# A graph-attention layer: gathers in waited bursts of two groups in place of spaced and paced gathers

## The chip, the cores and the metric

The kernel runs on one core of one Trainium2 chip. The metric is the device time of one launch in microseconds (us), the median over runs. The engines are TensorE (PE, with its weight loads PEld), VectorE (DVE), ScalarE (ACT), GpSimd (POOL) and SyncE (SP); DMAs are issued from SP, ACT and POOL.

## The reference

One layer of edge attention on a graph of 6250 nodes and 100,000 edges, 8 heads of 12, with a residual and a norm. The edges are sorted by destination, the sources are random.

```python
Q_h = (x @ Wq + bq).reshape(N, H, D)
K_h = (x @ Wk + bk).reshape(N, H, D)
V_h = (x @ Wv + bv).reshape(N, H, D)
E = (edge_attr @ We + be).reshape(-1, H, D)
score = K_h[src] * Q_h[dst] / sqrt(D) * E
score = exp(clip(score.sum(-1, keepdims=True), -5.0, 5.0))
wV = segment_sum(V_h[src] * score, dst)
Z = segment_sum(score, dst)
return layernorm(x + (wV / (Z + 1e-6)).reshape(N, H * D))
```

## The kernel before

**Tables.** TensorE computes keys, values and queries of all nodes in 50 tiles of 128 nodes; ScalarE copies them out of PSUM and SP stores them in two tables in HBM, kv_table (rows of 192 floats, 768 bytes) and q_table. Meanwhile GpSimd gathers the x rows of the sources of the first 8 groups, and TensorE computes their keys and values straight from them, so that these groups need no table.

**Groups.** The edges are taken in 196 groups (`GROUPS`) of 4 tiles (`GROUP_TILES`) of 128 edges; the last group has 2 tiles, 782 tiles in all. For each tile GpSimd issues one indirect DMA (L493, in `gather`) that fetches 128 rows of kv_table by the tile's source numbers into the ring `kv` of 16 groups (`KV_RING`). Each ring slot has its own semaphore, `e_kv[slot]`, which a gather raises by 16 when its rows have landed.

**What each engine does for a group.** TensorE, in this order in one iteration of its loop: `features_and_queries` (L1023 edge features, L1030 queries of the edges by a one-hot product), for the group two before it `turn` (L1041, transposes of their product), and for the group five before it `segment_sums` (L1055). ScalarE makes the one-hot matrix (L588, L591), copies the features (L597) and takes the exponentials (L602, L603). VectorE multiplies queries and features (L751), multiplies that with the gathered keys (L761, `times_keys`; this is the operation that waits for `e_kv`), sums over the heads (L768), clips (L775), weighs the gathered values (L782, `weigh_v`, which raises `e_msg`) and adds the sums of a window of 80 nodes to the accumulator (L797). SP loads edge features, relative rows and query windows, in rings of 8 groups. TensorE raises `e_e` (L1023), `e_q` (L1030), `e_turn` (L1041) and `e_seg` (L1055), once for each group.

**The order on GpSimd.** It has nothing to do but the gathers. After every gather stands a spacer (L500, in `space`): a memset of a tile that no one reads, which also waits for the memset before it. Groups 0 to 7 (`EARLY`) gather x rows; then GpSimd waits until all tables are stored; groups 8 to 15 go out without a wait; groups 16 to 31 wait, once for each group, until the slot's old contents have been used (`e_msg`); from group 32 on (`PACED_FROM`) each of the four gathers of a group waits for a signal of TensorE:

```python
pool.wait_ge(*((e_seg, group - 3), (e_e, ahead + 1),
               (e_q, ahead + 1), (e_turn, group + 1))[t])
```

where `ahead` is `group + 2`. The other engines' rows are ordered by hand; finished nodes are normalised and stored while the groups go on (`steps_at`). Of the three paths (`by_path`) these inputs take the streamed one, `windowed(True)`.

Of the kernel before, what the change touches and what calls it, by code (L numbers as in the profile page):

```python
# [31 lines left out]
F32 = mybir.dt.float32  # L32
# [7 lines left out]
P = 128  # L40
# [6 lines left out]
GROUP_TILES = 4  # L47
GROUP = GROUP_TILES * P
GROUPS = -(-N_EDGES // GROUP)
# [4 lines left out]
QUADS = GROUPS // QUAD  # L54
WINDOW = 80
EARLY = 8
PACED_FROM = 32

NODE_TILES = -(-N_NODES // P)
TABLE_TILES = NODE_TILES + 1  # L60
# [19 lines left out]
KV_RING, EA_RING, REL_RING, QWIN_RING, PICK_RING, MSG_RING = 16, 8, 8, 8, 4, 4  # L80
# [9 lines left out]
TURNED, WEIGHED, SUMMED, ADDED = 2, 3, 5, 5  # L90
# [4 lines left out]
def tiles_of(group):  # L95
    return min(GROUP_TILES, TILES - group * GROUP_TILES)


def edges_in(tile):
    return min(P, N_EDGES - tile * P)  # L100
# [37 lines left out]
def build(nc, xT, x_rows, src_cols, dst_cols, dst_rows, eaT, weights, biases, ones, out):  # L138
# [9 lines left out]
    assert FINISHED_AFTER[STREAMED_STEPS - 2] + LAG_DIVIDE < GROUPS + 1 == FINISHED_AFTER[STREAMED_STEPS - 1] + LAG_DIVIDE  # L148
    assert STREAMED_STEPS == STEPS - 1 and ADDED == 5 and TURNED == 2 and WEIGHED == 3
    assert SUMS * FINAL_TILES + WINDOW <= 512 and LAG_TRANSPOSE == SUMMED + 2  # L150
    assert KV_RING > 2 * SUMMED and PACED_FROM >= KV_RING
    assert EARLY < KV_RING and tiles_of(EARLY) == GROUP_TILES


# [6 lines left out]
    with ExitStack() as ctx:  # L161
        def sb(name, shape, dt):
            return ctx.enter_context(nc.sbuf_tensor(name, shape, dt))
# [4 lines left out]
        def sem(name):  # L168
            return ctx.enter_context(nc.semaphore(name))
# [66 lines left out]
        rows_f = acc_t[0:PAIRS, 0:2 * GROUP].rearrange("p (j e) -> p j e", j=2)  # L236


        spacer = sb("spacer", [P, 128], F32)
        g_src = sb("g_src", [P, GROUP_TILES], U32)  # L240
        g_dst = sb("g_dst", [P, GROUP_TILES], U32)
        g_dst_f = sb("g_dst_f", [P, GROUP_TILES], F32)
# [58 lines left out]
        e_kv = [sem(f"e_kv{i}") for i in range(KV_RING)]  # L301
# [5 lines left out]
        e_e = sem("e_e")  # L307
        e_q = sem("e_q")
# [3 lines left out]
        e_turn = sem("e_turn")  # L312
# [4 lines left out]
        e_msg = sem("e_msg")  # L317
        e_seg = sem("e_seg")
        e_acc = sem("e_acc")
        e_space = sem("e_space")  # L320
        g_free = sem("g_free")
        g_idx = sem("g_idx")
        g_step = sem("g_step")
# [31 lines left out]
        def path_of(eng):  # L355
            eng.wait_ge(r_ready, 1)
            return eng.value_load(path_i[0:1, 0:1], min_val=GENERAL, max_val=STREAMED)
# [6 lines left out]
        def all_tables_stored(eng):  # L364
            for i in range(UNITS_IN_RING):

                eng.wait_ge(d_table[i], 32 * len(range(i, UNITS, UNITS_IN_RING)))

        def by_path(eng, path, windowed, general):

            with eng.If(path == STREAMED):
                windowed(True)
            with eng.Else():
                with eng.If(path == WINDOWED):
                    windowed(False)
                with eng.Else():
                    general()
# [103 lines left out]
        @block.gpsimd  # L481
        def _(pool):
            nc.gpsimd.memset(ident[:], 0.0).then_inc(c_id0, 1)
            pool.wait_ge(c_id0, 1)
            nc.gpsimd.affine_select(out=ident[:], in_=ident[:], compare_op=ALU.not_equal, fill=1.0, base=0,
                                    pattern=[[-1, P]], channel_multiplier=1).then_inc(c_ident, 1)
            nc.gpsimd.iota(iota_i[:], pattern=[[1, SPAN]], base=0, channel_multiplier=0).then_inc(c_iota, 1)
            nc.gpsimd.iota(part_i[:], pattern=[[1, 1]], base=0, channel_multiplier=1).then_inc(c_iota, 1)

            def gather(rows, table, group, t, semaphore):  # L490
                tile = group * GROUP_TILES + t
                n = edges_in(tile)
                pool.indirect_dma_start(rows[0:n, :], None, table,  # L493
                                        bass.IndirectOffsetOnAxis(ap=src_idx[0:n, tile:tile + 1], axis=0)
                                        ).then_inc(semaphore, 16)

            def space(tile):
                if tile:
                    pool.wait_ge(e_space, tile)
                nc.gpsimd.memset(spacer[:], 0.0).then_inc(e_space, 1)  # L500

            pool.wait_ge(l_src_early, 16)
            for group in range(EARLY):
                for t in range(GROUP_TILES):
                    gather(kv[:, group, t, 0:DIM], x_rows, group, t, e_kv[group])
                    space(group * GROUP_TILES + t)
            pool.wait_ge(l_src, 16)
            all_tables_stored(pool)
            path = path_of(pool)

            def windowed(streamed):
                for group in range(EARLY, GROUPS):
                    slot, ahead = group % KV_RING, min(group + 2, GROUPS - 1)
                    if KV_RING <= group < PACED_FROM:
                        pool.wait_ge(e_msg, group - KV_RING + 1)
                    for t in range(tiles_of(group)):
                        if group >= PACED_FROM:
                            pool.wait_ge(*((e_seg, group - 3), (e_e, ahead + 1), (e_q, ahead + 1), (e_turn, group + 1))[t])
                        gather(kv[:, slot, t, :], kv_table, group, t, e_kv[slot])
                        space(group * GROUP_TILES + t)  # L520

            def general():
                pool.wait_ge(l_dst, 16)
                pool.wait_ge(x_kv, 2 * EARLY)
                with pool.Fori(0, GROUPS) as group:
                    pool.wait_ge(g_free, group + 1)
                    cols = bass.ds(group * GROUP_TILES, GROUP_TILES)
                    nc.gpsimd.tensor_copy(g_src[:], src_idx[:, cols]).then_inc(g_idx, 1)
                    nc.gpsimd.tensor_copy(g_dst[:], dst_idx[:, cols]).then_inc(g_idx, 1)
                    pool.wait_ge(g_idx, group * 2 + 2)  # L530
                    pool.sem_inc(g_step, 1)
                    for t in range(GROUP_TILES):
                        pool.indirect_dma_start(
                            kv[:, 0, t, :], None, kv_table,
                            bass.IndirectOffsetOnAxis(ap=g_src[:, t:t + 1], axis=0)).then_inc(g_gather, 16)
                        pool.indirect_dma_start(
                            g_q[:, t, :], None, q_table,
                            bass.IndirectOffsetOnAxis(ap=g_dst[:, t:t + 1], axis=0)).then_inc(g_gather, 16)

            by_path(pool, path, windowed, general)  # L540


# [605 lines left out]
```

## Time and profile before

| | |
|---|---|
| median of 2 runs | 1071.3 us (1071.09 to 1071.5) |
| span of the profiled execution | 1231.7 us |
| time of the profiled execution around its span | not shown by the profile |
| GpSimd busy | 919.8 us (75%) |
| TensorE busy, mean granted clock | 824.3 us (67%), 0.81 |
| VectorE busy | 595.7 us (48%) |
| ScalarE busy | 457.8 us (37%) |
| rows gathered by GpSimd's queue | 75.28 MB, 23.9% of the 16 DMA engines' span |

The profile is of one execution. Its rows give the start and length of each instruction; the length of a gather on GpSimd is the making of its descriptors, and its rows land later. The granted clock is TensorE's, 1.0 for 2.4 GHz and 0.5 for 1.2 GHz. The profiled execution is 160 us longer than the timed ones.

### The profile page before, as it was taken

To read this page: it belongs to the slowest core of one execution; us is meant where nothing else is said; L and a number is where in the kernel's file an instruction comes from. 1 tells how busy PE (TensorE), PEld (TensorE's weight loads), DVE (VectorE), ACT (ScalarE), POOL (GpSimd) and SP (SyncE) were. 2 spreads that over 40 slices of the span, in tenths; PEclk is the share of its full clock that TensorE was granted. 3 is DMA by queue.
4 is the path that set the end of the run, shared out by engine and by line. 5 is a ranking of instruction groups with operands and counts; after the bars stand their busy time and mean duration, and the time that the engine had idled before them with its cause. 6 is when DMAs were issued, how large, how long until landed. Compare 5 with 4: busy or idle time off the path is not lost.

```text
span 1231.7 us, 13818 instructions
## 1 busy us (share of the span) xinstructions
PE 824.3 (67%) x3375; PEld 455.9 (37%) x3375; DVE 595.7 (48%) x1583; ACT 457.8 (37%) x1094; POOL 919.8 (75%) x1572
## 2 busy tenths in 40 slices
PE   6518565986676666667676667666767676776763
PEld 4415232543343333333333334333333333333433
DVE  5104344954444464445444545445554545454645
ACT  3206232743343343333333334333434343433331
POOL 8882777167878778778787787887777877877783
PEclk9757787988877888887888787887878877878885
DMA  9922344454545445445444444444444444444321
GB/s 245 277 77 77 104 126 109 137 145 120 144 116 138 125 112 131 125 111 127 122 121 125 108 135 117 120 132 120 111 130 125 128 127 112 121 130 126 92 77 51
DMA packets 124525, 153.29 MB, mean 124 GB/s; under 512 B 57885, under 2 KB 92191, under 8 KB 124436
## 3 DMA queue, kind: packets, MB, share of 16 engines
q0 software_dynamic: 37008, 75.28, 23.9%
q1 hardware_dynamic: 80608, 73.74, 21.7%
q10 hardware_dynamic: 6822, 3.31, 1.0%
q8 instruction: 31, 0.51, 0.2%
q14 instruction: 56, 0.46, 0.1%
HBM read 142.26 MB, written 9.98 MB: 124 GB/s over the span
## 4 chain that ended last, share of the span: by engine, by line
POOL 37%; PE 22%; issue 16%; another core or an unknown queue 10%; DVE 6%; DMA 6%; ACT 2%; SPq 0%; DVEq 0%; POOLq 0%
POOL kv L493 30%; POOL spacer L500 7%; DMA kv<-kv_table,src_idx 5%; PE ps_eq L1030 4%; PE ps_eq L1023 4%; PE ps_qe_seg L1055 3%; PE ps_last L1055 3%; PE ps_eq_qe L1023 2%; PE ps_qe_seg L1041 2%; PE ps_eq_qe L1030 1%; PE ps_eq_qe L1041 1%; DVE ps_last L768 1%; DVE node_stage L743 1%; DMA w_all<-biases_in 1%
## 5 line engine op out<-in xcount | busy, mean ns | idle before, releaser
L493 POOL DMA_INDIRECT kv<-kv_table,src_idx x750 | 714.2, 952 | 285.5 <-issue 114.7
L602 ACT ACTIVATE ps_last<-clipped 128x32 f32<-128x32 f32 x196 | 39.4, 201 | 542.4 <-issue 397.2
L1030 PE MATMUL ps_eq<-pick_t,q_win 128*96 128x512 f32 (+1 forms) x262 | 169.5, 735 | 78.7 <-ACT e_t L597 58.4
L761 DVE TENSOR_TENSOR kq<-kv,ps_qe_seg 128x384 f32<-128x384 f32 x98 | 53.9, 550 | 260.7 <-DMA kv<-kv_table,src_idx 195.7
L1023 PE MATMUL ps_eq<-ea,w_all 128*96 128x512 f32 (+1 forms) x262 | 172.5, 747 | 8.1 <-issue 7.4
L500 POOL MEMSET spacer<- 128x128 f32 x782 | 172.8, 221 | 2.7 <-remote 2.2
L761 DVE TENSOR_TENSOR kq<-kv,ps_eq_qe 128x384 f32<-128x384 f32 x98 | 54.1, 552 | 238.3 <-DMA kv<-kv_table,src_idx 175.5
L1055 PE MATMUL ps_qe_seg<-node_stage 128*104 128x80 f32 x784 | 116.2, 306 | 54.5 <-issue 28.9
L1055 PE MATMUL ps_last<-node_stage 128*104 128x80 f32 x780 | 108.2, 292 | 49.3 <-issue 24.2
L588 ACT ACTIVATE distance<-rel_bc,neg_part 80x512 bf16<-80x512 bf16 x196 | 138.4, 706 | 1.8 <-issue 0.6
L1055 PEld LDWEIGHTS ps_qe_seg<-node_stage 128*104 128x104 f32 x784 | 105.2, 218 | 64.6 <-issue 49.6
L591 ACT ACTIVATE pick_t<-distance 80x512 f32<-80x512 bf16 x196 | 123.2, 629 | 6.2
L1055 PEld LDWEIGHTS ps_last<-node_stage 128*104 128x104 f32 x780 | 97.7, 205 | 58.0 <-issue 33.5
L1030 PEld LDWEIGHTS ps_eq<-pick_t,q_win 128*96 128x96 f32 x262 | 46.4, 199 | 195.0 <-issue 194.4
L597 ACT COPY e_t<-ps_eq 96x512 f32<-96x512 f32 x131 | 74.3, 567 | 92.6 <-remote 58.2
L768 DVE TENSOR_REDUCE ps_last<-kq 128x32 f32<-128x384 f32 x196 | 107.6, 549 | 0.1
L782 DVE TENSOR_TENSOR node_stage<-kv,ps_last 128x384 f32<-128x384 f32 x196 | 106.3, 542 | 0.0
L1041 PE MATMUL ps_qe_seg<-ident,qe_t 96*128 96x96 f32 x390 | 60.0, 285 | 65.9 <-issue 41.2
L1030 PE MATMUL ps_eq_qe<-pick_t,q_win 128*96 128x512 f32 x130 | 82.6, 722 | 31.7 <-issue 15.8
L1041 PEld LDWEIGHTS ps_qe_seg<-ident,qe_t 96*128 96x128 f32 x390 | 48.3, 164 | 146.1 <-issue 103.4
L751 DVE TENSOR_TENSOR qe_t<-e_t,ps_eq 96x512 f32<-96x512 f32 x131 | 88.3, 674 | 17.5 <-PE ps_eq L1030 8.9
L1041 PEld LDWEIGHTS ps_eq_qe<-ident,qe_t 96*128 96x128 f32 x392 | 48.3, 160 | 125.9 <-issue 92.3
(90 smaller groups left out, 788.2 us busy)
## 6 DMA issues: line engine op xcount, KB each, us to landing
ea<-ea_t_in SPq DMA_DIRECT2D x196, 192.0 KB
rel_bc<-rel_rows_dram SPq DMA_DIRECT2D x196, 80.0 KB
kv<-kv_table,src_idx POOLq DMA_INDIRECT x750
q_win<-q_table SPq DMA_DIRECT2D x196, 30.0 KB
kv_table<-node_stage SPq DMA_DIRECT2D x5, 576.0 KB
x_both<-x_t_in SPq DMA_DIRECT2D x5, 480.0 KB, 8.9
x_both<-x_rows_in ACTq DMA_DIRECT2D x10, 240.0 KB
out<-node_stage SPq DMA_DIRECT2D x11, 192.0 KB
```

Of the source, the lines that this page charges most:

```text
L493: pool.indirect_dma_start(rows[0:n, :], None, table, bass.IndirectOffsetOnAxis(ap=src_idx[0:n, tile:tile + 1], axis=0)).then_inc(semaphore ...
L500: nc.gpsimd.memset(spacer[:], 0.0).then_inc(e_space, 1)
L588: nc.scalar.activation(distance[:, b, 0:n], rel_bc[:, slot, 0:n], ACT.Abs, bias=neg_part[0:WINDOW, :]).then_inc(e_dist, 1)
L591: nc.scalar.activation(pick_t[0:WINDOW, group % 3, 0:n], distance[:, b, 0:n], ACT.Relu, bias=1.0, scale=-1.0).then_inc(e_pt, 1)
L751: nc.vector.tensor_tensor(qe_t[:, group % QE_RING, 0:n], e_t[:, group % 2, 0:n], ps_eq[(2 * group + 1) % 3][0:DIM, 0:n], ALU.mult).then_in ...
L761: nc.vector.tensor_tensor(kq[:, group % 2, 0:n, :], kv[:, slot, 0:n, 0:DIM], ps_qe[group % 2][:, 0:n * DIM].rearrange("p (t d) -> p t d", ...
L768: nc.vector.tensor_reduce(score[:, group % 2, 0:n, :], kq[:, group % 2, 0:n, :].rearrange("p t (h d) -> p t h d", h=HEADS), axis=AX_X, op= ...
L782: nc.vector.tensor_tensor(m[:, :, 0:DIM].rearrange("p t (h d) -> p t h d", h=HEADS), kv[:, group % KV_RING, 0:n, DIM:2 * DIM].rearrange("p ...
L1023: nc.tensor.matmul(ps_eq[2 * group % 3][0:DIM, 0:n], w_e, ea[:, slot, 0:n], start=True, stop=True).then_inc(e_e, 1)
L1030: nc.tensor.matmul(ps_eq[(2 * group + 1) % 3][0:DIM, 0:n], q_win[:, slot, :], pick_t[:, group % 3, 0:n], start=True, stop=True).then_inc(e ...
L1041: last = nc.tensor.transpose(ps_qe[group % 2][:, t * DIM:(t + 1) * DIM], qe_t[:, group % QE_RING, t * P:(t + 1) * P], ident[0:DIM, 0:DIM])
L1055: last = nc.tensor.matmul(ps_seg[group % 2][0:SUMS, 0:WINDOW], msg[:, group % MSG_RING, t, :], pick[:, group % PICK_RING, t, :], start=(t ...
```

## The change

The spacers and the four signals of TensorE go. Gathers go out in bursts of two groups (`BURST`), eight gathers one behind the other, and behind each burst GpSimd waits until both groups have landed (`landed`, on `e_kv` of both slots). The wait for the ring slot (`e_msg`) stands ahead of every group from 16 on. Behind the last burst there is no wait for its landing. The other four engines' programs are unchanged.

```diff
-PACED_FROM = 32
+BURST = 2
...
-        spacer = sb("spacer", [P, 128], F32)
...
-        e_space = sem("e_space")
...
-            def space(tile):
-                if tile:
-                    pool.wait_ge(e_space, tile)
-                nc.gpsimd.memset(spacer[:], 0.0).then_inc(e_space, 1)
+            def landed(group, tiles):
+
+                slot = group % KV_RING
+                before = sum(tiles_of(g) for g in range(slot, group, KV_RING))
+                pool.wait_ge(e_kv[slot], 16 * (before + tiles))
 
             pool.wait_ge(l_src_early, 16)
             for group in range(EARLY):
                 for t in range(GROUP_TILES):
                     gather(kv[:, group, t, 0:DIM], x_rows, group, t, e_kv[group])
-                    space(group * GROUP_TILES + t)
+                if group % BURST == BURST - 1:
+                    for g in range(group - BURST + 1, group + 1):
+                        landed(g, GROUP_TILES)
...
                 for group in range(EARLY, GROUPS):
-                    slot, ahead = group % KV_RING, min(group + 2, GROUPS - 1)
-                    if KV_RING <= group < PACED_FROM:
+                    slot = group % KV_RING
+                    if group >= KV_RING:
                         pool.wait_ge(e_msg, group - KV_RING + 1)
                     for t in range(tiles_of(group)):
-                        if group >= PACED_FROM:
-                            pool.wait_ge(*((e_seg, group - 3), (e_e, ahead + 1), (e_q, ahead + 1), (e_turn, group + 1))[t])
                         gather(kv[:, slot, t, :], kv_table, group, t, e_kv[slot])
-                        space(group * GROUP_TILES + t)
+                    if group % BURST == BURST - 1 and group < GROUPS - 1:
+                        for g in range(group - BURST + 1, group + 1):
+                            landed(g, GROUP_TILES)
```

On GpSimd at the start of the program (the gathers of x rows), the kernel before has a spacer behind each gather:

```order
L493 DMA kv<-x_rows_in,src_idx 128x96 [waits l_src_early]
L500 MEMSET spacer 128x128
L493 DMA kv<-x_rows_in,src_idx 128x96
L500 MEMSET spacer 128x128 [waits e_space]
L493 DMA kv<-x_rows_in,src_idx 128x96
L500 MEMSET spacer 128x128 [waits e_space]
```

The changed kernel has eight gathers in a row, and the first of each next eight waits for the landing of two groups:

```order
L491 DMA kv<-x_rows_in,src_idx 128x96 [waits l_src_early]
L491 DMA kv<-x_rows_in,src_idx 128x96 x7
L491 DMA kv<-x_rows_in,src_idx 128x96 [waits e_kv1,e_kv0]
L491 DMA kv<-x_rows_in,src_idx 128x96 x7
L491 DMA kv<-x_rows_in,src_idx 128x96 [waits e_kv3,e_kv2]
L491 DMA kv<-x_rows_in,src_idx 128x96 x7
```

The spacers are gone, and the waits of the early part moved from the spacer's own semaphore to the landings.

On GpSimd in the steady stage, the kernel before has for one group four gathers that wait for TensorE's signals, with the spacers between them:

```order
L493 DMA kv<-kv_table,src_idx 128x192 [waits e_seg]
L500 MEMSET spacer 128x128 [waits e_space]
L493 DMA kv<-kv_table,src_idx 128x192 [waits e_e]
L500 MEMSET spacer 128x128 [waits e_space]
L493 DMA kv<-kv_table,src_idx 128x192 [waits e_q]
L500 MEMSET spacer 128x128 [waits e_space]
L493 DMA kv<-kv_table,src_idx 128x192 [waits e_turn]
L500 MEMSET spacer 128x128 [waits e_space]
```

The changed kernel has there, for three groups (`e_msg` is the ring slot, `e_kv` with a number the landing of a slot):

```order
L491 DMA kv<-kv_table,src_idx 128x192 [waits e_msg,e_kv3,e_kv2]
L491 DMA kv<-kv_table,src_idx 128x192 x3
L491 DMA kv<-kv_table,src_idx 128x192 [waits e_msg]
L491 DMA kv<-kv_table,src_idx 128x192 x3
L491 DMA kv<-kv_table,src_idx 128x192 [waits e_msg,e_kv5,e_kv4]
L491 DMA kv<-kv_table,src_idx 128x192 x3
```

No wait for TensorE is left there; every second group begins with the wait for the landing of the two before it, and all gathers behind it stand in the same queue.

## Rows read from the trace of the kernel before

**Rows 1.** The page: busy time of each engine, and the chain that ended last
```profile
PE 824.3 (67%) x3375; PEld 455.9 (37%) x3375; DVE 595.7 (48%) x1583; ACT 457.8 (37%) x1094; POOL 919.8 (75%) x1572
...
POOL kv L493 30%; POOL spacer L500 7%; DMA kv<-kv_table,src_idx 5%; PE ps_eq L1030 4%; PE ps_eq L1023 4%; PE ps_qe_seg L1055 3%; PE ps_last L1055 3%; PE ps_eq_qe L1023 2%; PE ps_qe_seg L1041 2%; PE ps_eq_qe L1030 1%; PE ps_eq_qe L1041 1%; DVE ps_last L768 1%; DVE node_stage L743 1%; DMA w_all<-biases_in 1%
```
**Rows 2.** Groups of GpSimd (busy, mean ns | idle before); one line by duration (least/median/longest)
```profile
L493 POOL DMA_INDIRECT kv<-kv_table,src_idx x750 | 714.2, 952 | 285.5 <-issue 114.7 <-remote 58.7 <-PE ps_qe_seg L1055 49.7
L500 POOL MEMSET spacer<- 128x128 f32 x782 | 172.8, 221 | 2.7 <-remote 2.2
...
L493 POOL DMA_INDIRECT kv<-kv_table,src_idx x750: 881/952/968, 50.7 to 1215.3; - x188
```
**Rows 3.** Timeline, steady stage: start, length, engine, operation, [idle before <-releaser]
```profile
700.07 0.95 POOL L493 DMA_INDIRECT kv<-kv_table,src_idx  x1 [0.17 <-issue]
...
701.02 0.22 POOL L500 MEMSET spacer<- 128x128 f32 x1
...
701.40 0.95 POOL L493 DMA_INDIRECT kv<-kv_table,src_idx  x1 [0.17 <-issue]
...
704.08 0.95 POOL L493 DMA_INDIRECT kv<-kv_table,src_idx  x1 [0.16 <-issue]
...
706.65 0.55 DVE L761 TENSOR_TENSOR kq<-kv,ps_eq_qe 128x384 f32<-128x384 f32 x1 [2.48 <-DMA kv<-kv_table,src_idx]
```
**Rows 4.** Waits: who waited for whom, us in total, times, longest
```profile
DVE kq L761 <- DMA kv<-kv_table,src_idx: 371.2, 131, 5.4
...
POOL kv L493 <- remote: 58.7, 36, 2.2
...
POOL kv L493 <- PE ps_qe_seg L1055: 49.7, 10, 35.0
```
**Rows 5.** Timeline, the first gather of the program
```profile
4.58 1.12 POOL L493 DMA_INDIRECT kv<-x_rows_in,src_idx  x1 [2.50 <-DMA src_idx<-src_cols_in]
```
**Rows 6.** Timeline, the last gather and the product that waits for it
```profile
1215.28 0.88 POOL L493 DMA_INDIRECT kv<-kv_table,src_idx  x1 [0.17 <-issue]
...
1217.58 0.35 DVE L761 TENSOR_TENSOR kq<-kv,ps_qe_seg 128x192 f32<-128x192 f32 x1 [0.97 <-DMA kv<-kv_table,src_idx]
```
**Rows 7.** Timeline, a ring slot comes free and GpSimd's gather follows
```profile
150.14 0.54 DVE L782 TENSOR_TENSOR node_stage<-kv,ps_last 128x384 f32<-128x384 f32 x1
...
150.95 0.95 POOL L493 DMA_INDIRECT kv<-kv_table,src_idx  x1 [5.17 <-DVE node_stage L782]
```
**Rows 8.** The start: timeline; DMA issues (us to landing); engines, clock, DMA share by stretch
```profile
24.72 5.61 DVE L691 MEMSET acc_t<- 104x6656 f32 x1 [1.45 <-issue]
...
28.68 2.57 POOL L493 DMA_INDIRECT kv<-x_rows_in,src_idx  x1 [0.17 <-issue]
...
50.68 0.95 POOL L493 DMA_INDIRECT kv<-kv_table,src_idx  x1 [0.53 <-issue]
...
x_both<-x_t_in SPq DMA_DIRECT2D x5, 480.0 KB, 8.9
...
10.00:20.00 10.00, 8.44 (x21) 6.20 (x22) 7.77 (x12) 2.56 (x4) 8.92 (x13) 1.00 1.00 242
```
**Rows 9.** Timeline, TensorE's steps of a group: two at the lower clock, then four at full clock
```profile
699.97 1.94 PE L1023 MATMUL ps_eq<-ea,w_all 128*96 128x512 f32 x2
...
716.08 1.65 PE L1055 MATMUL ps_qe_seg<-node_stage 128*104 128x80 f32 x8 [0.90 <-issue]
...
709.69 1.04 PE L1023 MATMUL ps_eq<-ea,w_all 128*96 128x512 f32 x2
...
710.90 1.07 PE L1030 MATMUL ps_eq_qe<-pick_t,q_win 128*96 128x512 f32 x2 [0.17 <-ACT e_t L597]
...
708.56 0.49 PE L1041 MATMUL ps_eq_qe<-ident,qe_t 96*128 96x96 f32 x4
...
708.92 0.93 PE L1055 MATMUL ps_last<-node_stage 128*104 128x80 f32 x8
```
**Rows 10.** Steady stage: busy (count) of PE, PEld, DVE, ACT, POOL; clock; DMA share; GB/s
```profile
254.00:1214.00 960.00, 663.71 (x2660) 350.75 (x2658) 474.85 (x1284) 356.85 (x871) 763.45 (x1305) 0.81 0.46 121
```

More of the change, by code:

```diff
@@ L150, in build @@
     assert SUMS * FINAL_TILES + WINDOW <= 512 and LAG_TRANSPOSE == SUMMED + 2
-    assert KV_RING > 2 * SUMMED and PACED_FROM >= KV_RING
+    assert KV_RING > 2 * SUMMED
     assert EARLY < KV_RING and tiles_of(EARLY) == GROUP_TILES
```

## The prediction

> **What bounds the kernel now.** I read the views from the whole to the single instruction. The page first: GpSimd (POOL) is busy 75% of the span, TensorE 67%, VectorE 48% [rows 1], and the chain that ended last has 30% on the gathers and 7% on the spacers, both on GpSimd [rows 1]. The reader should see that no line of another engine has more than 4% there. Then the groups of GpSimd: 750 gathers from kv_table at 952 ns (the other 32 take the x rows) and 782 spacers at 221 ns [rows 2]. Then the timeline of one group in the steady stage: a gather starts at 700.07, the next at 701.40, the fourth of the group at 704.08, so one every 1.336 us: 0.95 gather, 0.22 spacer, 0.17 of gap that nothing explains ("issue"), although the next gather was already queued [rows 3]. The list of waits says who pays: VectorE's product with the keys waits 371 us for gathers to land, in 131 waits [rows 4].
>
> Is GpSimd really the bound of the timed runs, which take 1071.3 us where the profiled execution's span is 1231.7? GpSimd's idle before its table gathers is 285.5 us [rows 2]; 750 gaps of 0.165 are 124 of it, and the other 162 are stalls of the profiled execution: a ring not yet free or TensorE not yet far enough at the start (50 us on TensorE in 10 waits, the longest 35) and 36 waits of 1.6 us on average whose cause the trace does not name [rows 4]. 1231.7 less 162 is 1070, which is the median. The same from below: start of the first gather 4.58, 782 x 1.336 = 1044.8 less the last spacer and its gap, 0.4, and 15.5 from the end of the last gather (1216.16) to the end of the span give 1064.4 [rows 3, 5 and 6]. So I read the timed runs as a gapless row of gather and spacer on GpSimd, with 6.9 us for everything else. All sums below are made in that row and the 6.9 us are kept; against the profiled span itself the same differences stand on top of 162 us of stalls, part of which may go.
>
> **The change part by part.**
> Spacers: 782 memsets of 0.22 leave, with their share of the gaps. Two gathers in a row without a spacer do not occur in this trace, so the new step of a gather has to be bounded. Lower end: 0.95, the gather alone. Upper end from the same rows: 1.336, as if the spacing were needed anyway. In between lies 0.95 + 0.17 = 1.12, if the gap belongs to the gather and not to the spacer. The gap stands ahead of gathers and never ahead of a spacer [rows 3], so I take 1.12.
>
> Pacing: the waits on TensorE's four signals leave. In the gapless row they cost nothing; in the profiled execution the one long wait ahead of group 32 goes. The wait for the ring slot (e_msg) now stands ahead of every group; GpSimd is the slow engine, the slot was left sixteen groups earlier, so it costs nothing once the consumers have caught up.
>
> The landing waits: new, one per eight gathers, 4 in the early part (x rows), then 93, none behind the last two groups. What is queued behind one is all of GpSimd: the next eight gathers. From the end of a group's last gather to VectorE's start on it I read 705.03 to 706.65 = 1.62 [rows 3] and, in the drain, 1216.16 to 1217.58 = 1.42 [rows 6]. A gather released by a semaphore starts 0.27 after the release (150.68 to 150.95) [rows 7], where VectorE's start already holds a like reaction. From the end of a burst to the next gather that makes 1.5 to 1.9 in the quiet stage. The burst sends its rows in a shorter time and waits for the slowest of two groups, so I take 2.0. The upper end is that of a loaded queue: a load at the start lands in 8.9 us, with the DMA engines at a share of 1.00 [rows 8]. That end counts in full only for the four early bursts, for which I take 5.
>
> The Trainium skill (DMA: Bandwidth & Descriptors, "Anatomy of one DMA — SWDGE (gpsimd) path") gives 2.0 us plus bytes over 436 GB/s for one such DMA, nearly all of it the receipt of the last write, and so speaks against a wait for each burst. For 96 KB that is an estimate of 2.2 us from the issue, where the trace has 2.57 from the start of the gather (704.08) to VectorE's start [rows 3]. By the page a burst would be 0.3 us shorter, some 30 us over the kernel; by the row it is not, and I go by the row.
>
> A burst: 7 x 1.12 + 0.95 + 2.0 = 10.79 us for two groups. Eight gathers with spacers take 8 x 1.336 = 10.69. The whole gain of eight spacers, 1.7 us, is thus taken by one wait for the landing.
>
> The sum: first gather 4.58; four early bursts of 7 x 1.12 + 0.95 + 5.0 = 13.8, together 55.2, so that the tables' gathers begin at about 60.3 with the 0.5 of path loading (before: 50.68 [rows 8]); 93 x 10.79 = 1003.5; the last six gathers 5 x 1.12 + 0.95 = 6.6; the tail 15.5. That is 1085.9 against 1064.4 for before by the same way, so +21.5, and with the median 1071.3 + 21.5 = 1093 us, 2.0% slower. This mechanism's own range: 0.5 us more or less per wait is 46 us, so 1050 to 1140.
>
> Do the others keep up? TensorE's four steps of a group at full clock take 1.04 + 1.07 + 0.49 + 0.93 = 3.5 us, at the lower clock the first takes 1.94 and the last 1.65, 1.8 times as long, which makes 6.4 for the group [rows 9]; VectorE's work is 475 us in the 960 us of the steady stage, which hold about 653 gathers (1305 instructions of GpSimd, every second a spacer), so 2.9 us a group [rows 10]. At 5.4 us a group both have room unless TensorE stays at the lower clock. The landings then come 4.5 and 6.3 us apart in turn (4 x 1.12; 10.8 less that) instead of evenly; I cost that at nothing, since both are above the 3.5 us that TensorE needs at full clock.
>
> **The rivals.**
> A. The gap goes with the spacer. Then a gather behind a gather starts after 0.95 to 1.0. For it: the spacer's own start follows the gather's end without any gap [rows 3]. Against it: the gap stands ahead of the gather, with work queued. There are 684 such steps (7 in each of 97 bursts, 5 in the last); 0.12 to 0.17 less each are 82 to 116 us: 977 to 1011, about 990. It decides below a step of 1.06.
> B. The ending on the far slow side: a gather right behind a gather takes longer on GpSimd, since the descriptors of its predecessor are still being taken when it wants to write its own (a gather lands 1.6 us after its end [rows 3], so two or three are on the way at once). For it: a gather of the loaded start lasted 2.57 instead of 0.95 [rows 8]. Against: it stood beside VectorE's long memset of the sums (24.72, 5.61 us) [rows 8], and the 750 table gathers have their least, median and longest at 881, 952 and 968 ns [rows 2]. Its price: from a step of 1.12 to 1.34 it is 0.22 x 684 = 150 us, so 1243; at a step of 1.2, 1148. It decides above a step of 1.15 (then the burst is over 11 us).
> C. TensorE falls to 1.2 GHz in the pauses. For it: mean granted clock 0.81 in the steady stage [rows 10] although the groups came evenly. If two thirds of the groups went at 6.4, TensorE would take 5.4 and be the bound; at 6.4 throughout the 196 groups alone are 1254 us, and more with the start. Then GpSimd would wait for ring slots, the landing waits would be met already, and the change would not do what it says. Against: at 6.4 us a group TensorE would be busy without a pause, and the mean of 0.81 between the levels 0.5 and 1.0 shows that the clock came back each time in the steady stage.
>
> **How the numbers follow.** Forecast mechanism 0.45, A 0.28, B 0.22, C 0.05. A measurement of this kernel tells about 2%, 21 us, from no change. The forecast's 1050 to 1140 puts 0.04 below 1050, 0.19 within, 0.22 above 1093; A gives 0.26 faster and 0.02 within; B and C 0.27 slower. Together: faster 0.30, within 2% 0.21, slower 0.49. The range leaves out the lower part of A with cheap waits and the upper part of B: 975 to 1215, and the likeliest one's own is 1050 to 1140.
>
> **What would show each step.** In the profile after, no L500 group, and the gather of table rows still at about 950 ns; starts of gathers in a burst 1.12 apart (A: 0.97, B: 1.2 and more); the idle before gathers put down to the landing of kv, about 97 waits of 1.5 to 2.0; the first table gather at about 60 us; VectorE's wait for kv still the largest in its list. I am wrong if the step in a burst is not 1.12, if the waits are under 1.4 or over 2.5, or if GpSimd no longer waits for landings because TensorE or a full ring holds it.

## The result and the profile after

The changed kernel takes 1261.4 us (median of two runs, 1258.0 and 1264.8) against 1071.3 before: 1.177 times as long, 95% interval 1.170 to 1.185. The forecast was 1093, the stated range 975 to 1215, so the result lies outside it. Slower was the right side; the size was wrong by 168 us. Timed twice more (e5 and e16 below), the ratio came out at 1.181 (1.176 to 1.185) and 1.182 (1.178 to 1.185).

The page of the changed kernel: busy time by engine, and the costliest group. It answers to [rows 1 and 2].

```profile
PE 861.7 (69%) x3375; PEld 474.6 (38%) x3375; DVE 594.3 (47%) x1583; ACT 452.2 (36%) x1094; POOL 742.2 (59%) x790
...
L491 POOL DMA_INDIRECT kv<-kv_table,src_idx x750 | 708.5, 945 | 465.6 <-issue 456.5
```

The gather itself is as long as before (945 ns, before 952), and GpSimd has 178 us less to do, which is the 173 us of spacers and 6 us of the gathers. But its idle time ahead of the table gathers has gone from 285.5 to 465.6 us, in an execution with a span of 1256.1. GpSimd is busy 59%, TensorE 69%, and still no other engine is the bound, as the waits show (waiting instruction, releaser: us in total, times, longest; the row of VectorE answers to [rows 4]):

```profile
DVE kq L762 <- DMA kv<-kv_table,src_idx: 595.4, 174, 6.1
POOL kv L491 <- issue: 465.0, 775, 5.3
...
POOL kv L491 <- DMA kv<-x_rows_in,src_idx: 19.5, 3, 8.8
...
POOL kv L491 <- DMA kv<-kv_table,src_idx: 9.1, 3, 3.2
```

VectorE waits 595 us for gathers to land, 371 before. Of 93 landing waits behind table gathers the list puts three down to the landing. The rest stand under "issue", with a longest of 5.3 us, so the name of the releaser misleads here; the timeline does not. One border between two bursts in the steady stage, GpSimd and then VectorE's product with the keys of the group that landed last (start, length, engine, operation, [idle before]):

```profile
705.90 0.95 POOL L491 DMA_INDIRECT kv<-kv_table,src_idx  x1 [0.30 <-issue]
707.15 0.94 POOL L491 DMA_INDIRECT kv<-kv_table,src_idx  x1 [0.30 <-issue]
...
710.63 0.56 DVE L762 TENSOR_TENSOR kq<-kv,ps_qe_seg 128x384 f32<-128x384 f32 x1 [3.13 <-DMA kv<-kv_table,src_idx]
...
711.34 0.94 POOL L491 DMA_INDIRECT kv<-kv_table,src_idx  x1 [3.24 <-issue]
712.59 0.95 POOL L491 DMA_INDIRECT kv<-kv_table,src_idx  x1 [0.30 <-issue]
```

Two things are to be seen, both unlike the forecast. Inside a burst the gathers start 1.25 us apart, with 0.30 us between one and the next: that is 0.09 less than with a spacer (1.336, [rows 3]), not 0.22. And at the border GpSimd stands still for 3.24 us: VectorE starts 2.54 us after the end of the last gather, and GpSimd, which waits for the same rows, starts 0.71 us later still. Over the whole trace the gap behind the first gather of a burst is 0.385 us and the other six are 0.305, so 0.316 on average; the one at a border is 2.74 on average (this border is a long one).

The sum from this trace: the first table gather starts at 68.28; 93 bursts of 8 x 0.945 + 7 x 0.316 + 2.74 = 12.51 are 1164; the last six gathers 7.2; the tail 17. That is 1256, against a span of 1256.1.

```profile
68.28 0.94 POOL L491 DMA_INDIRECT kv<-kv_table,src_idx  x1 [3.20 <-issue]
...
DMA to landing us min/median/max: 2.4/2.7/6.4
```

The steady stage, engines busy, clock, DMA share and GB/s, answers to [rows 10]: the same stretch holds 616 gathers where 653 ran before, and TensorE has 302 of 960 us free at a granted clock of 0.78.

```profile
254.00:1214.00 960.00, 657.58 (x2508) 347.32 (x2508) 447.54 (x1208) 336.22 (x830) 581.36 (x616) 0.78 0.42 114
```

### The profile page after: what moved, and what is told of

Read it like the earlier page. It is cut to its first block and busy times, and to the rows that moved or that the text cites. A ratio compares the mean times of both kernels' runs of the same rounds, so it can differ in the third digit from the quotient of the medians.

```text
span 1256.1 us, 13133 instructions
## 1 busy us (share of the span) xinstructions
PE 861.7 (69%) x3375; PEld 474.6 (38%) x3375; DVE 594.3 (47%) x1583; ACT 452.2 (36%) x1094; POOL 742.2 (59%) x790
## 5 line engine op out<-in xcount | busy, mean ns | idle before, releaser
L491 POOL DMA_INDIRECT kv<-kv_table,src_idx x750 | 708.5, 945 | 465.6 <-issue 456.5
L762 DVE TENSOR_TENSOR kq<-kv,ps_eq_qe 128x384 f32<-128x384 f32 x98 | 54.2, 553 | 411.2 <-DMA kv<-kv_table,src_idx 411.2
L1042 PE MATMUL ps_eq_qe<-ident,qe_t 96*128 96x96 f32 x392 | 63.1, 293 | 201.1 <-DVE kq L762 201.0
L1056 PE MATMUL ps_last<-node_stage 128*104 128x80 f32 x780 | 137.8, 346 | 90.5 <-DVE acc_t L798 79.9
L1024 PE MATMUL ps_eq<-ea,w_all 128*96 128x512 f32 (+1 forms) x262 | 185.5, 799 | 7.9 <-DVE qe_t L752 6.3
L1056 PEld LDWEIGHTS ps_last<-node_stage 128*104 128x104 f32 x780 | 122.8, 251 | 105.8 <-DVE node_stage L783 94.3
L1056 PE MATMUL ps_qe_seg<-node_stage 128*104 128x80 f32 x784 | 94.7, 267 | 35.2 <-DVE acc_t L798 24.7
L1056 PEld LDWEIGHTS ps_qe_seg<-node_stage 128*104 128x104 f32 x784 | 86.6, 184 | 41.6 <-DVE node_stage L783 29.4
L1024 PE MATMUL ps_eq_qe<-ea,w_all 128*96 128x512 f32 x130 | 93.4, 809 | 3.5 <-DVE qe_t L752 3.5
L744 DVE TENSOR_TENSOR node_stage<-ps_last,rel_f 128x320 f32<-128x320 f32 x196 | 94.5, 482 | 0.5 <-ACT ps_last L603 0.5
L1042 PEld LDWEIGHTS ps_qe_seg<-ident,qe_t 96*128 96x128 f32 x390 | 54.6, 175 | 98.8 <-issue 62.4
```

The source lines that it names most:

```text
L491: pool.indirect_dma_start(rows[0:n, :], None, table, bass.IndirectOffsetOnAxis(ap=src_idx[0:n, tile:tile + 1], axis=0)).then_inc(semaphore ...
L744: nc.vector.tensor_tensor(pick[:, group % PICK_RING, 0:n, :], window_iota.unsqueeze(1).to_broadcast([P, n, WINDOW]), rel.unsqueeze(2).to_b ...
L762: nc.vector.tensor_tensor(kq[:, group % 2, 0:n, :], kv[:, slot, 0:n, 0:DIM], ps_qe[group % 2][:, 0:n * DIM].rearrange("p (t d) -> p t d", ...
L1024: nc.tensor.matmul(ps_eq[2 * group % 3][0:DIM, 0:n], w_e, ea[:, slot, 0:n], start=True, stop=True).then_inc(e_e, 1)
L1042: last = nc.tensor.transpose(ps_qe[group % 2][:, t * DIM:(t + 1) * DIM], qe_t[:, group % QE_RING, t * P:(t + 1) * P], ident[0:DIM, 0:DIM])
L1056: last = nc.tensor.matmul(ps_seg[group % 2][0:SUMS, 0:WINDOW], msg[:, group % MSG_RING, t, :], pick[:, group % PICK_RING, t, :], start=(t ...
```

## The experiments

All kernels compute the whole output. One thing has to be known before the numbers: the kernel before takes 1071 to 1073 us on some chips and 1214 or 1228 on others. Each experiment was timed beside it on its own chip, and I call them the 1072 chips (e5 to e12, e16 to e18, and the changed kernel's own) and the slower chips (e1 to e4 at 1214, e13 to e15 at 1228). The profile of before with its span of 1231.7 is like the slower ones; the runs of 1071.3 are of the other kind. The experiments ran on five chips (2, 4 and 14 of the one kind, 10 and 13 of the other; that of the first pair is not on record), each of them met once, so it is not shown whether a chip stays of its kind. Some kernels ran on both kinds.

**What each step of the forecast costs, on the 1072 chips.**

e9, the changed kernel without its landing waits (pacing and spacers gone as well):

```diff
-                if group % BURST == BURST - 1:
-                    for g in range(group - BURST + 1, group + 1):
-                        landed(g, GROUP_TILES)
...
-                    if group % BURST == BURST - 1 and group < GROUPS - 1:
-                        for g in range(group - BURST + 1, group + 1):
-                            landed(g, GROUP_TILES)
```

> The changed kernel without its landing waits, once more, since the first four runs were on a chip where the kernel before takes 1214 us and the next four on one where it takes 1072. Theory 1 (the row of steps) on a chip where the kernel before takes 1072: 4.6 + 782 x 1.25 + 22 = 1005, no unnamed waits. On a chip where it takes 1214 or so: 1320 again, with some 500 us of unnamed waits of ScalarE.

Measured: 1006.95 us, ratio 0.940 (0.937 to 0.942). This is the fastest kernel of the study, 6% faster than the one before. Its group of gathers, its timeline and its steady stage:

```profile
L491 POOL DMA_INDIRECT kv<-kv_table,src_idx x750 | 709.7, 946 | 233.1 <-issue 229.8 <-DVE node_stage L777 3.4
```

```profile
703.08 0.95 POOL L491 DMA_INDIRECT kv<-kv_table,src_idx  x1 [0.30 <-issue]
704.33 0.95 POOL L491 DMA_INDIRECT kv<-kv_table,src_idx  x1 [0.30 <-issue]
```

```profile
254.00:980.00 726.00, 534.07 (x2366) 282.61 (x2364) 425.19 (x1156) 315.07 (x782) 549.19 (x581) 0.88 0.53 141
```

An unbroken row of 1.25 us steps: 5.2 + 782 x 1.25 + 17 of tail is 1000, and the loaded start adds 5, against a span of 1005.3. No ring slot and no landing holds it (3.4 us in all). So the gapless row in which the forecast did its sums does exist on these chips, and the gather has a step of 1.25 in it.

e11, the kernel before without its spacers, pacing by TensorE kept:

```diff
-                    space(group * GROUP_TILES + t)
...
-                        space(group * GROUP_TILES + t)
```

> The kernel before without its spacers, once more. Theory 1 on a chip where the kernel before takes 1072: 782 x 0.085 = 67 us less, about 1005, so that the spacers are a pure loss there. On a chip where it takes 1214: 1232 again.

Measured: 1007.32 us, ratio 0.940 (0.937 to 0.943), the same as e9. So on these chips the pacing costs nothing once the spacers are gone, as the forecast said, and the spacers cost 782 x (1.336 - 1.25) = 67 us; measured are 64.

e5 and e16, the changed kernel again, beside e6 to e8 and e17 and e18:

> The changed kernel as it is, timed beside the kernel before on one chip, since the kernel before took 1071 us in the first pair and 1214 on the chip of the last four runs. If the first pair's distance is the change's own, 1.177 again; if only the kernel before differs from chip to chip (its profile shows 162 us of stalls, the changed kernel's almost none), this one stays at 1261 and the ratio is 1.04 on the chip of the last runs.

> The changed kernel. Where the kernel before takes 1072: 1265, ratio 1.18. Where it takes 1214 to 1228: the same 1265 if its landing waits of 2.7 us free the signals every time (ratio 1.03), over 1300 with unnamed waits if not.

Measured: 1268.6 and 1267.2 us. Against e9 the landing waits alone are worth 260 us. In e5's trace a border is 2.87 us on average: 93 x (2.87 - 0.30) = 239 us between table gathers, 93 x 0.08 = 7 for the longer gap behind the first gather of a burst, and 18 us earlier, since the first table gather starts at 68.0 there and at 50.3 in e9. That makes 264; the two profiled runs, 1269.6 and 1007.2, lie 262 apart.

e6, bursts of four groups (`BURST = 4`), so half as many landing waits:

```diff
-BURST = 2
+BURST = 4
```

> The changed kernel with bursts of four groups (sixteen gathers) and half as many landing waits. Theory 1 (GpSimd is a row of steps of 1.25 and waits of 3.0): 48 waits of 3.0 less the step that stands in their place, 84 us less: about 1175. Theory 2 (TensorE's signals are held back while gathers follow each other for long, and a pause of GpSimd frees them): sixteen gathers are 20 us, long enough to hold signals; the waits of ScalarE for unnamed causes come back (0 here, 536 us without landing waits) and the time stays above 1200.

Measured: 1139.9 us, ratio 1.063 (1.060 to 1.067). A border is 2.94 us here; 46 of them at 2.94 - 0.30 are 121, the longer first gaps 4, and the first table gather is 6 us later than in e9: 1138, against 1137.4 in the profiled run. The loss goes with the number of waits.

e7 and e12, a memset of 1024 columns in place of each landing wait, and e8 and e17, three of them. Is it the landing that costs, or would any pause do the same?

```diff
+                nc.gpsimd.memset(resting[:], 0.0).then_inc(e_rest, 1)
...
-                    for g in range(group - BURST + 1, group + 1):
-                        landed(g, GROUP_TILES)
+                    rest()
```

> The changed kernel with a memset of 1024 columns (about 1.1 us) behind each burst of eight gathers in place of the landing wait: a pause in making descriptors, but no wait for landings. Theory 1: 97 x 1.9 us less than 1261, about 1080. Theory 2: if one microsecond frees the signals, the same 1080; if what frees them is that all gathers have landed or that GpSimd stands idle, over 1250 with hundreds of us of unnamed waits.

> The pause of one memset of 1024 columns per eight gathers, once more. On a chip where the kernel before takes 1072: 1085 again. On one where it takes 1214: if a pause of 1.1 us frees TensorE's held signals, under 1150; if it takes landed gathers or an idle GpSimd, over 1250 with hundreds of us of unnamed waits.

> The same with three such memsets, about 3.3 us, longer than the landing takes. Theory 1: the same row as the changed kernel, 1261 within 3%. Theory 2: if a pause in descriptors is what counts, 1261 and no unnamed waits; if GpSimd must be idle, over 1300.

> Three memsets per eight gathers in place of the landing wait. Where the kernel before takes 1072: 1278. Where it takes 1214 to 1228: 1278 and no unnamed waits if the length of the pause in gathers is what frees the signals; over 1320 with unnamed waits if it takes the landing or an idle GpSimd.

Measured: 1085.0 and 1084.6 us with one memset; 1278.5 and 1278.6 with three. The timeline of the one and of the other:

```profile
709.15 0.95 POOL L493 DMA_INDIRECT kv<-kv_table,src_idx  x1 [0.30 <-issue]
710.09 0.98 POOL L502 MEMSET resting<- 128x1024 f32 x1
711.23 0.95 POOL L493 DMA_INDIRECT kv<-kv_table,src_idx  x1 [0.17 <-issue]
```

```profile
710.28 2.99 POOL L503 MEMSET resting<- 128x1024 f32 x3
713.43 0.95 POOL L493 DMA_INDIRECT kv<-kv_table,src_idx  x1 [0.15 <-issue]
```

The border is 1.13 us in the first (710.10 to 711.23) and 3.14 in the second. Over the 0.30 of a plain gap, 93 borders between table gathers add 77 and 264 us to e9's 1007, and the first table gather starts 0.6 us earlier and 7.5 later than in e9 (49.7, 57.8 and 50.3): 1084 and 1279. Both are within 1 us of the profiled runs, 1083.9 and 1278.8. A pause of a given length costs the same whether GpSimd waits for a landing or fills it with a memset; nothing about the landing is dear but its length (and the 0.08 us behind the first gather). The rows also show where the small price of the spacer comes from: a memset starts at the gather's very end (709.15 + 0.95 is 710.10), and the gap ahead of the next gather shrinks from 0.30 to 0.17. Part of the memset lies in a gap that is there anyway.

e10 and e18, each landing wait names only the last group of its burst, one semaphore in place of two:

```diff
-                    for g in range(group - BURST + 1, group + 1):
-                        landed(g, GROUP_TILES)
+                    landed(group, GROUP_TILES)
```

> The changed kernel, but each landing wait waits for the second group of the burst alone (one semaphore for two; with the ring slot two for three). If the 0.73 us between the landing and the next gather is made up of one more wait instruction per semaphore, it falls to about 0.5 and the time by 97 x 0.2 = 20 us or so, to 1245; if 0.73 is the price of any wait for a landing, it stays at 1261. Both theories on held signals: no unnamed waits.

> Landing wait for the second group of the burst alone. Where the kernel before takes 1072: 1227. Where it takes 1214 to 1228: 1227 if a pause of 2.2 us is enough, over 1260 with unnamed waits if it is not.

Measured: 1226.7 and 1218.1 us, ratios 1.145 (1.139 to 1.151) and 1.136 (1.132 to 1.140), e18 49 us below e16 of its own chip. The border in the timeline of e10, and GpSimd's waits:

```profile
708.22 0.94 POOL L491 DMA_INDIRECT kv<-kv_table,src_idx  x1 [0.30 <-issue]
...
711.45 0.56 DVE L760 TENSOR_TENSOR kq<-kv,ps_qe_seg 128x384 f32<-128x384 f32 x1 [2.85 <-DMA kv<-kv_table,src_idx]
...
711.68 0.94 POOL L491 DMA_INDIRECT kv<-kv_table,src_idx  x1 [2.52 <-DMA kv<-kv_table,src_idx]
```

```profile
POOL kv L491 <- DMA kv<-kv_table,src_idx: 233.4, 93, 3.5
POOL kv L491 <- issue: 211.6, 685, 3.0
```

GpSimd now starts 0.23 us behind VectorE's start, not 0.71, and the trace names the landing as the releaser in all 93 cases. From the landing record to the next gather it is 0.26 us, against 0.73 with two landing waits and 0.86 with four (e6). So the second wait on GpSimd costs about half a microsecond after everything has landed. The longer gap behind the first gather of a burst goes with it too: in both traces of this kernel all seven gaps are about 0.305. 93 x (0.47 + 0.08) = 51 us, of 49 measured between e18 and e16; that e10 is 9 us above e18 comes from later landings (2.25 against 2.16 us after the last gather) and a later first table gather (68.4 against 66.3).

**The slower chips: are spacers and pacing good for something there?**

e1, the kernel of e9; e2, the changed kernel with spacers put back; e3, the kernel of e11; e4, the kernel before without the four waits on TensorE (first the cut of e2, then that of e4):

```diff
+                nc.gpsimd.memset(spacer[:], 0.0).then_inc(e_space, 1)
...
+                        space(group * GROUP_TILES + t)
```

```diff
-                        if group >= PACED_FROM:
-                            pool.wait_ge(*((e_seg, group - 3), (e_e, ahead + 1), (e_q, ahead + 1), (e_turn, group + 1))[t])
```

> The changed kernel without its landing waits: unspaced gathers, only the ring-slot wait. Theory 1 (GpSimd is a row of gathers; in a burst a gather now takes a step of 1.25 us, and each landing wait costs 3.0 us from the end of the burst, 2.3 for the landing and 0.73 to start again): 4.6 + 782 x 1.25 + 22 = about 1005 us, steps of 1.25 throughout. Theory 2 (rival B of the prediction: gathers behind gathers without pause become slow once more than a few are on the way, and the waits only bound that): over 1071 us, with gathers or gaps well over 1.25 once twenty or so are out.

> The changed kernel with the spacers put back behind every gather, landing waits kept. Theory 1: 0.085 us more per step (1.336 for 1.25) on 684 steps, 58 us: about 1320. Theory 2 (spacing protects the gathers): landings come sooner and the time falls under 1261.

> The kernel before without its spacers, TensorE's signals kept. Theory 1: steps of 1.25, 782 x 0.085 = 67 us less: about 1005. Theory 2: the spacers are needed, 1071 or more.

> The kernel before with the ring-slot wait ahead of every group in place of TensorE's signals, spacers kept. Theory 1: the signals are met already in the timed runs: 1071 within 1%. Theory 2 (the pacing spreads the gathers and that is worth something): slower than 1090.

Measured, against 1214.2 for before on that chip: e1 1319.6 (ratio 1.086, 1.081 to 1.091), e2 1323.0 (1.089, 1.083 to 1.094), e3 1231.8 (1.014, 1.010 to 1.018), e4 1285.7 (1.058, 1.054 to 1.062). The kernel of e9 and e1, one text, is thus 6% faster than before on one kind of chip and 9% slower on the other. What stops e1 is seen in its timeline, all engines (TensorE's product into `ps_eq`, the gathers, and ScalarE's copy of that product):

```profile
697.50 1.04 PE L1018 MATMUL ps_eq<-ea,w_all 128*96 128x512 f32 x2
...
700.28 1.04 PE L1018 MATMUL ps_eq_qe<-ea,w_all 128*96 128x512 f32 x2
...
703.36 0.18 DVE L770 TENSOR_SCALAR clipped<-ps_last 128x32 f32<-128x32 f32 x1
704.01 0.95 POOL L491 DMA_INDIRECT kv<-kv_table,src_idx  x1 [0.30 <-issue]
...
710.26 0.95 POOL L491 DMA_INDIRECT kv<-kv_table,src_idx  x1 [0.30 <-issue]
712.81 0.24 DVE L792 TENSOR_TENSOR acc_t<-acc_t,ps_qe_seg 104x80 f32 x1 [9.27 <-remote]
714.13 0.58 ACT L592 COPY e_t<-ps_eq 96x512 f32<-96x512 f32 x1 [14.83 <-remote]
...
714.85 1.99 PE L1025 MATMUL ps_eq<-pick_t,q_win 128*96 128x512 f32 x2 [13.54 <-ACT e_t L592]
...
717.48 0.94 POOL L491 DMA_INDIRECT kv<-kv_table,src_idx  x1 [6.28 <-DVE node_stage L777]
```

TensorE's product ends at 698.5. ScalarE, idle since 699.3, copies it at 714.1; the trace has the rise of the semaphore (`e_e`) for which it waits at 714.11. From 703.5 to 712.8 nothing runs on TensorE, VectorE or ScalarE, while six gathers go out without a break (704.01 to 710.26); here the others go on only when the ring is full and GpSimd has stopped. What waits is always a reader of something TensorE made, and the trace cannot name its releaser ("remote"): all 173 such waits of e1 are for a semaphore that TensorE raises, and none of the twelve traces from the 1072 chips has any. A pause of GpSimd is not all that ends them: of ScalarE's 71 in the row below, 42 end in a pause of over 0.6 us and 29 while gathers go out. The same row of the waits of ScalarE's copy in e1, then e2, e4 and the kernel before:

```profile
ACT e_t L592 <- remote: 536.1, 71, 15.9
```

```profile
ACT e_t L607 <- remote: 15.8, 5, 5.1
```

```profile
ACT e_t L595 <- remote: 564.0, 87, 14.9
```

```profile
ACT e_t L597 <- remote: 79.4, 26, 13.6
```

Spacers alone (e4) do not prevent it. Waits for TensorE's own signals (before; e3, 54.2 us) or for landings after each eight gathers (e2) do, for the most part. What e2 takes, 1323, is what the bare row gives: the changed kernel's 1261 to 1269 on the 1072 chips and 684 x 0.085 = 58 us of spacers (at a border the spacer lies within the wait) are 1319 to 1327.

e13, e14 and e15 ask what kind of break is enough there: the 1 us memset of e7, the bursts of four groups of e6, and landing waits that lag by one burst (they wait for the burst before the last, so that eight gathers are always on the way):

```diff
-                        for g in range(group - BURST + 1, group + 1):
+                        for g in range(group - 2 * BURST + 1, group - BURST + 1):
```

> The pause of one memset of 1024 columns per eight gathers. On a chip where the kernel before takes 1072: 1085. On one that holds TensorE's signals (before 1214): under 1150 if a short pause of the gathers frees them, over 1250 with hundreds of us of unnamed waits if it takes the landing.

> Bursts of four groups with landing waits. On a chip where the kernel before takes 1072: 1140. On one that holds the signals: above 1200 with unnamed waits of over 100 us if sixteen gathers in a row are long enough to hold them; 1140 if they are not.

> Bursts of two groups, but behind each burst GpSimd waits for the landing of the burst before it, which has long landed. By the row of terms: no pause is left, 1007 as without landing waits where the kernel before takes 1072, if a wait that is met costs nothing; up to 0.5 us for each of 97, 1055, if the wait instructions themselves cost. On a chip that holds the signals: 1320 as without landing waits.

Measured, against 1227.5 for before: 1289.5 (ratio 1.050, 1.046 to 1.054), 1299.0 (1.058, 1.049 to 1.067) and 1348.1 (1.098, 1.088 to 1.108), with 578, 579 and 561 us of ScalarE's waits on "remote". None of the three prevents the late signals. What differs in e2 is that GpSimd stands still for some 2.8 us after each eight gathers; it also has spacers, and with 13.2 us for eight gathers it is the slowest row of all. A low rate of gathers, and not the break, is thus a rival that no run rules out, though the mean rate alone does not decide: the kernel before and e13 took 12.4 and 12.6 us for eight gathers in their traces, with 79 and 578 us of these waits. Whether a memset of that length does as well is not shown either: e8 and e17 both ran on 1072 chips. The changed kernel itself was never run on a slower chip, so that it would avoid the held-back signals there is an inference from e2.

## Why the prediction was wrong, step by step

- **What bounds the kernel.** Right. The timed runs of before are a gapless row on GpSimd (no trace of before from a 1072 chip is kept, so this rests on the sums); e9 and e11 shorten that row and nothing else, and gain what the row says. Laying 162 us of stalls on the profiled execution was right in the sum too, but I took them for accidents of one execution. They look like those of the slower chips (85 unnamed waits for TensorE's signals stand in that trace), on which all kernels here that let GpSimd run freely lose far more.
- **The step of 1.12 in a burst.** The step that failed first. I gave the 0.17 gap to the gather and let the whole spacer of 0.22 go. Measured is 1.25 (0.946 + 0.30): the spacer lay partly in a gap that is 0.30 long without it. With the mean gap of 0.316 the step is 1.26, 0.14 more than forecast, over the 656 steps between table gathers in bursts 92 us.
- **The landing wait of 2.0 us.** The second. I had it from VectorE's start in the quiet stage (1.42 to 1.62), counted a reaction like GpSimd's 0.27 as already in it, and rounded up for the slowest rows of two groups. Measured is 2.74: the slowest rows of the burst land about 2.0 after its last gather, and GpSimd needs 0.73 more to come out of its waits. VectorE's start holds next to no reaction: GpSimd starts 0.73 after the landing and 0.71 after VectorE, so VectorE starts 0.02 after it. The 2.0 thus paid for the landing and left nothing for the restart, and the 0.27 of [rows 7] is that of one wait, not of several. 93 x 0.74 = 69 us.
- **The early part and the tail.** 68.3 where 60.3 was forecast, 8 us: the step again (4), one gather of 2.8 us (2), and waits of 8.8, 5.3, 5.5 and 3.2 where four of 5 were counted (3); tail 1.4 us more. With these the forecast's own sum of 1085.9 becomes 1085.9 + 92 + 69 + 8 + 1 = 1256, the span of 1256.1. Of the 6.9 us kept on top of it for everything else, 1.9 are there (the profiled run took 1258.0); the rest had its like in the start, which the 68.3 already holds.
- **The page's rule** that such a DMA takes 2.0 us plus its bytes over 436 GB/s (Trainium skill, DMA: Bandwidth & Descriptors, "Anatomy of one DMA — SWDGE (gpsimd) path") would have made the burst shorter still. The trace does not agree: the row at 2.57 was nearer, and the changed kernel's median is 2.7 from the gather's start. The measurement decides.
- **"The others keep up", at no cost.** Right: TensorE free for 302 of 960 us at a clock of 0.78, and GpSimd never held by a ring slot in a way that shows.
- **Rival A** (the gap goes): wrong by sign; the gap grew from 0.17 to 0.30. **Rival B** (a gather behind a gather takes longer): the measured step of 1.25 lies above the 1.15 at which the prediction lets B decide, and its time at that step would have been 1182, the nearest of all. But its mechanism is not what the trace shows: gathers are 945 ns long, shorter than before (952), and 750 table gathers in a row in e9 keep 0.30 between them, without the growth that I would expect of a queue that fills. Why the gap is 0.30 behind a gather and 0.17 behind a memset is not shown. **Rival C** (TensorE at the lower clock as bound): did not occur.
- **The range.** It took the step's uncertainty and the wait's as alternatives. Both came out at their high end together, 12.51 for a burst where 10.79 was forecast, and the end of the range was made with only one of them high.

## What to carry to other kernels

On the engine that bounds the kernel, a filler between two DMA issues costs less than its own length, because a gap stands there anyway (0.085 of 0.22 us here), while a wait for a landing costs everything from the last issue to the restart (2.4 us over the plain gap, 93 times); count such a wait with the restart, and with one semaphore rather than two. Removing pacing and waits altogether gave 1007 us on one kind of chip and 1320 on the other, so compare a kernel with its rival on the same chip, and look whether the profile that you read is of the kind of chip that the timed runs were. A version without spacers but with the pacing (e3, e11) is the safest of the changes tried: 0.940 on the one, 1.014 on the other, where nothing that ran was faster than the kernel before.

## What the runs showed of the hardware

- A gather behind a gather on GpSimd starts 0.30 us after its end, behind a memset 0.15 to 0.17 us; the memset itself starts at once. The gather's own length hardly depends on it (0.946 and 0.952).
- Restart of GpSimd after a landing: 0.26 us with one landing semaphore, 0.73 with two, 0.86 with four (each with the ring's semaphore beside them); with two and four the gap behind the next gather is 0.08 us longer as well. VectorE starts 0.02 us after the same landing. Why the second costs more than the third and fourth together stays open.
- On some chips signals from TensorE reach the other engines up to some 15 us late while gathers run without longer breaks; the product of 698.5 was read at 714.1, and the longest wait of ScalarE in e1 was 15.9. The same kernel takes 1319.6 us there and 1007 on the others. What delays them, what sets such chips apart, and how long a break must be was not settled.
